# Three tiles of features loaded ahead and the fourth in mid-run, with store slots of 87 instead of 65 pairs

## The chip, the core and the metric

The kernel runs on one core of a Trainium2 chip. The time is that of one execution on the device, in microseconds. The core has TensorE (PE, matrix products), ScalarE (ACT), VectorE (DVE), GpSimd (POOL), SyncE (SP, which here only issues transfers) and 16 DMA engines that move data between the main memory and the on-chip memory of 128 partitions.

## The reference

`r_x` has shape (512, 40, 128) and `W` (128, 128), both float32. Each of the 40 feature rows is projected, and then all 780 pairs (i, j) with i < j are multiplied element by element:

```python
proj = jnp.einsum('bnd,ed->bne', x, W)
out = proj[:, PAIR_I, :] * proj[:, PAIR_J, :]      # (512, 780, 128)
```

The input is 10.5 MB and the output 204.5 MB.

## The kernel before

The 512 rows are four tiles of 128, one row per partition. For each tile, `feats` holds 40 features of 128 numbers per partition. PE turns two features at a time (`turn`, L125) into PSUM, ACT copies them to `x_turned` (L174), PE multiplies them with the turned weights (`project`, L134), and ACT writes the result over the raw features in `feats` (L180). Such a pair of features is a group; there are 20 per tile, from the last features to the first.

DVE multiplies. The 780 pairs are ordered by i and then by j, so all pairs with one i and neighbouring j are one instruction (L197): feature i broadcast, times the features j to j + count - 1. The pairs are cut into chunks of 65, worked from the end of the list to its beginning, because the last features are projected first. A chunk fills one of three slots, `products0` to `products2`; where a chunk's edge lies within one i, that i's instruction is split in two. After a chunk DVE raises `chunk_ready`, SP issues one store of the slot (L107), and the store's landing raises `stored` of the slot, for which DVE waits before it fills that slot again (L196, L212). The first tile's chunks are written out instruction by instruction; the other three tiles are one loop body on DVE, `Fori(1, tiles)`, with the tile's number in a register.

SP issues everything in this order: the first tile in three loads, of features 36 to 39, 28 to 35 and 0 to 27 (L99), the other three tiles in one load each (L101), and then the 48 stores in the order of the chunks, each behind its wait (L106). PE waits for the parts of the first tile one by one, and then once for all three other tiles (L157), before it works on the second. All loads and stores are in one queue, q1. In what follows, tile 0 is the first and tile 3 the fourth.

Of the kernel before, what the change touches and what calls it, by code (L numbers as in the profile page):

```python
# [5 lines left out]
P = 128  # L6
FEATURES = 40
DIM = 128
PAIRS = FEATURES * (FEATURES - 1) // 2
FIRST_PAIR = [i * (FEATURES - 1) - i * (i - 1) // 2 for i in range(FEATURES)]  # L10

GROUP = 2
# [4 lines left out]
FIRST_LOADS = [(36, 40), (28, 36), (0, 28)]  # L17


SLOTS = 3  # L20
CHUNK = 65
CHUNKS = PAIRS // CHUNK
ROUNDS = CHUNKS // SLOTS

assert CHUNKS * CHUNK == PAIRS and ROUNDS * SLOTS == CHUNKS
assert GROUPS * GROUP == FEATURES and GROUPS % 2 == 0 and GROUP <= BANK_FEATURES


def group_range(group):
    return FEATURES - (group + 1) * GROUP, FEATURES - group * GROUP  # L30


def group_of(i):
    return (FEATURES - 1 - i) // GROUP


def chunk_range(k):
    return PAIRS - (k + 1) * CHUNK, PAIRS - k * CHUNK


def chunk_rows(low, high):

    rows = []
    for i in reversed(range(FEATURES - 1)):
        a, b = max(low, FIRST_PAIR[i]), min(high, FIRST_PAIR[i + 1])
        if a < b:
            rows.append((i, i + 1 + a - FIRST_PAIR[i], b - a, a - low))
    return rows


def pairwise_products(nc, x, w, out):
    fp32 = mybir.dt.float32
    ALU = mybir.AluOpType
    tiles = x.shape[0] // P
    assert x.shape[0] == tiles * P and 2 <= tiles <= 4

    with ExitStack() as ctx:  # L57
        def sbuf(name, shape):
            return ctx.enter_context(nc.sbuf_tensor(name, shape, fp32))

        def psum(name, shape):
            return ctx.enter_context(nc.psum_tensor(name, shape, fp32))

        def sem(name):
            return ctx.enter_context(nc.semaphore(name))


        feats = sbuf("feats", [P, tiles, FEATURES, DIM])
        products = [sbuf(f"products{s}", [P, CHUNK, DIM]) for s in range(SLOTS)]
        x_turned = [sbuf(f"x_turned{k}", [DIM, GROUP, P]) for k in range(2)]  # L70
        w_in = sbuf("w_in", [DIM, DIM])
        w_turned = sbuf("w_turned", [DIM, DIM])
        identity = sbuf("identity", [P, P])

        turned_ps = [psum(f"turned_ps{k}", [DIM, BANK_FEATURES, P]) for k in range(2)]
        proj_ps = [psum(f"proj_ps{k}", [P, BANK_FEATURES, DIM]) for k in range(2)]
# [3 lines left out]
        first_loaded = [sem(f"first_loaded{k}") for k in range(len(FIRST_LOADS))]  # L80

        tiles_loaded = sem("tiles_loaded")
        identity_zeroed = sem("identity_zeroed")
        identity_made = sem("identity_made")
        w_in_ps = sem("w_in_ps")
# [4 lines left out]
        proj_ready = sem("proj_ready")  # L90
        chunk_ready = sem("chunk_ready")
        stored = [sem(f"stored{s}") for s in range(SLOTS)]

        block = ctx.enter_context(nc.Block())

        @block.sync
        def _(sp):
            for k, (a, b) in enumerate(FIRST_LOADS):
                sp.dma_start(feats[:, 0, a:b, :], x[0:P, a:b, :]).then_inc(first_loaded[k], 16)  # L99
            for tile in range(1, tiles):  # L100
                sp.dma_start(feats[:, tile, :, :], x[tile * P:(tile + 1) * P, :, :]).then_inc(tiles_loaded, 16)  # L101

            for tile in range(tiles):
                for k in range(CHUNKS):
                    low, high = chunk_range(k)
                    sp.wait_ge(chunk_ready, tile * CHUNKS + k + 1)  # L106
                    sp.dma_start(out[tile * P:(tile + 1) * P, low:high, :],  # L107
                                 products[k % SLOTS][:, :, :]).then_inc(stored[k % SLOTS], 16)

            for slot in range(SLOTS):  # L110
                sp.wait_ge(stored[slot], 16 * tiles * ROUNDS)
# [8 lines left out]
        @block.tensor  # L120
        def _(pe):
            def turn(tile, group):
                a, b = group_range(group)
                for n in range(a, b):
                    last = pe.transpose(turned_ps[group % 2][:, n - a, :], feats[:, tile, n, :], identity[:, :])  # L125
                last.then_inc(group_turned, 1)

            def project(before, group):
                pe.wait_ge(x_turned_ready, before + (group + 1))
                if group >= 2:  # L130

                    pe.wait_ge(proj_ready, before + (group - 1))
                for k in range(GROUP):
                    last = pe.matmul(proj_ps[group % 2][:, k, :], x_turned[group % 2][:, k, :], w_turned[:, :],  # L134
                                     start=True, stop=True)
                last.then_inc(group_projected, 1)

            def last_banks_left(before):
                pe.wait_ge(proj_ready, before + GROUPS)

            pe.wait_ge(identity_made, 1)
            pe.wait_ge(w_loaded, 16)
            pe.transpose(w_ps[:, :], w_in[:, :], identity[:, :]).then_inc(w_in_ps, 1)  # L143

            starts = {group_of(b - 1): k for k, (a, b) in enumerate(FIRST_LOADS)}
            pe.wait_ge(first_loaded[0], 16)
            turn(0, 0)
            pe.wait_ge(w_ready, 1)
            for group in range(1, GROUPS):
                if group in starts:  # L150
                    pe.wait_ge(first_loaded[starts[group]], 16)
                turn(0, group)
                project(0, group - 1)
            project(0, GROUPS - 1)
            last_banks_left(0)

            pe.wait_ge(tiles_loaded, 16 * (tiles - 1))  # L157
            for tile in range(1, tiles):
                turn(tile, 0)
                for group in range(1, GROUPS):  # L160
                    turn(tile, group)
                    project(tile * GROUPS, group - 1)
                project(tile * GROUPS, GROUPS - 1)
                last_banks_left(tile * GROUPS)

        @block.scalar
        def _(act):
            act.dma_start(w_in[:, :], w).then_inc(w_loaded, 16)
            act.wait_ge(w_in_ps, 1)
            act.copy(w_turned[:, :], w_ps[:, :]).then_inc(w_ready, 1)  # L170

            def carry_turned(tile, group):
                act.wait_ge(group_turned, tile * GROUPS + group + 1)
                act.copy(x_turned[group % 2][:, :, :], turned_ps[group % 2][:, 0:GROUP, :]).then_inc(x_turned_ready, 1)  # L174

            def carry_projected(tile, group):

                a, b = group_range(group)
                act.wait_ge(group_projected, tile * GROUPS + group + 1)
                act.copy(feats[:, tile, a:b, :], proj_ps[group % 2][:, 0:GROUP, :]).then_inc(proj_ready, 1)  # L180

            for tile in range(tiles):
                carry_turned(tile, 0)
                for group in range(1, GROUPS):
                    carry_turned(tile, group)
                    carry_projected(tile, group - 1)
                carry_projected(tile, GROUPS - 1)

        @block.vector
        def _(dve):  # L190
            def multiply_chunk(tile, k, seen):

                for i, j, count, place in chunk_rows(*chunk_range(k)):
                    if group_of(i) >= seen:
                        seen = group_of(i) + 1
                        dve.wait_ge(proj_ready, tile * GROUPS + seen)  # L196
                    last = dve.tensor_tensor(  # L197
                        products[k % SLOTS][:, place:place + count, :],
                        feats[:, tile, i:i + 1, :].broadcast_to([P, count, DIM]),
                        feats[:, tile, j:j + count, :], ALU.mult)  # L200
                last.then_inc(chunk_ready, 1)
                return seen

            seen = 0
            for k in range(CHUNKS):
                if k >= SLOTS:
                    dve.wait_ge(stored[k % SLOTS], 16 * (k // SLOTS))
                seen = multiply_chunk(0, k, seen)
            with dve.Fori(1, tiles) as tile:  # L209
                seen = 0  # L210
                for k in range(CHUNKS):
                    dve.wait_ge(stored[k % SLOTS], 16 * ROUNDS * tile + 16 * (k // SLOTS))  # L212
                    seen = multiply_chunk(tile, k, seen)


# [19 lines left out]
```

## Time and profile before

| | |
|---|---|
| median of 3 runs | 505.68 us (505.66 to 505.83) |
| the profiled execution | 505.62 us |
| its span | 503.8 us |
| DVE busy | 433.6 us (86%) |
| PE, ACT busy | 63.4 us (13%), 54.2 us (11%) |
| queue q1, share of 16 DMA engines | 99.3% |
| bytes moved | 215.11 MB, 427 GB/s over the span |

The span is the stretch from the first to the last instruction of one profiled execution; what lies around it is 1.8 us. Busy shares say how full an engine is, not whether anyone waits for it. "Landing" is the moment at which a transfer's last completion count arrives. In the slices each digit is the busy share of a fortieth of the span (12.6 us), in tenths. A window's DMA share and rate are coarse where the window is short, since a packet is counted as a whole; that is why a share can stand above 1.

### The profile page before, as it was taken

How to read it: one execution, taken by the hardware profiler on the slowest of the kernel's cores; microseconds unless marked ns; L12 is line 12 of the kernel's file. 1: busy time of each engine (PE TensorE's matmuls, PEld its weight loads, DVE VectorE, ACT ScalarE, POOL GpSimd, SP SyncE). 2: the span in 40 equal slices, each digit the busy share in tenths (PEclk: the TensorE clock that was granted, in tenths of full speed). 3: DMA queues.
4: the chain of work that ended last, by engine and by line, in shares of the span. 5: the costliest groups of instructions: out<-in, count | busy, mean ns of one | idle time of the engine just before them, and what ended most of it. 6: DMA issues, size and time to landing. Idle time of an engine off the chain costs nothing.

```text
span 503.8 us, 1684 instructions
## 1 busy us (share of the span) xinstructions
PE 63.4 (13%) x481; PEld 57.6 (11%) x481; DVE 433.6 (86%) x196; ACT 54.2 (11%) x162; POOL 0.7 (0%) x6
## 2 busy tenths in 40 slices
PE   6659993000000000000000000000000000000000
PEld 5648982000000000000000000000000000000000
DVE  3987899899899989998898999899899989998930
ACT  5638982000000000000000000000000000000000
POOL 0000000000000000000000000000000000000000
PEclk9969997555555555555555555555555555555555
DMA  8999999999999999999999999999999999999997
GB/s 356 424 403 441 427 424 429 447 428 425 434 444 428 428 433 444 428 428 431 447 428 428 431 447 428 428 431 441 433 428 428 436 439 431 428 428 439 433 433 312
DMA packets 7926, 215.11 MB, mean 427 GB/s; under 512 B 880, under 2 KB 1008, under 8 KB 1264
## 3 DMA queue, kind: packets, MB, share of 16 engines
q1 hardware_dynamic: 7776, 214.96, 99.3%
q8 instruction: 4, 0.07, 0.0%
q10 hardware_dynamic: 144, 0.07, 0.0%
q14 instruction: 2, 0.02, 0.0%
HBM read 10.55 MB, written 204.47 MB: 427 GB/s over the span
## 4 chain that ended last, share of the span: by engine, by line
DMA 62%; DVE 25%; issue 5%; DVEq 2%; PE 1%; ACT 0%
DMA out_dram<-products 62%; DVE products L197 25%; DVEq L57 2%; DMA w_in<-in_L_rec_W_dram 1%; PE proj_ps L134 0%; PE turned_ps L125 0%; DVEq L197 0%; DVEq L196 0%; DVEq L209 0%; PE w_ps L143 0%; ACT feats L180 0%; DVEq L212 0%
## 5 line engine op out<-in xcount | busy, mean ns | idle before, releaser
L197 DVE TENSOR_TENSOR products<-feats 128x1280 f32 (+36 forms) x196 | 433.6, 2275 | 49.2 <-DMA out_dram<-products 41.1
L134 PE MATMUL proj_ps<-w_turned,x_turned 128*128 128x128 f32 x320 | 54.7, 295 | 0.6 <-ACT x_turned L174 0.5
L134 PEld LDWEIGHTS proj_ps<-w_turned,x_turned 128*128 128x128 f32 x320 | 43.3, 197 | 5.3 <-ACT x_turned L174 2.1
L125 PE MATMUL turned_ps<-identity,feats 128*128 128x128 f32 x160 | 31.7, 285 | 11.3 <-DMA feats<-in_r_x_dram 10.3
L174 ACT COPY x_turned<-turned_ps 128x256 f32<-128x256 f32 x80 | 30.0, 377 | 12.3 <-PE turned_ps L125 12.1
L180 ACT COPY feats<-proj_ps 128x256 f32<-128x256 f32 x80 | 29.8, 373 | 10.0 <-PE proj_ps L134 4.7
L125 PEld LDWEIGHTS turned_ps<-identity,feats 128*128 128x128 f32 x160 | 20.9, 148 | 12.3 <-issue 10.5
L170 ACT ACT_TABLE_LOAD x1 | 1.3, 1283 | 1.2 <-PEq L224 1.2
L143 PE MATMUL w_ps<-identity,w_in 128*128 128x128 f32 x1 | 0.4, 447 | 4.2 <-DMA w_in<-in_L_rec_W_dram 4.2
L143 PEld LDWEIGHTS w_ps<-identity,w_in 128*128 128x128 f32 x1 | 0.2, 182 | 4.2 <-issue 4.2
L170 ACT COPY w_turned<-w_ps 128x128 f32<-128x128 f32 x1 | 0.3, 266 | 2.3 <-PE w_ps L143 2.3
L117 POOL TENSOR_SCALAR_AFFINE_SELECT identity<-identity 128x128 f32<-128x128 f32 x1 | 0.3, 294 | 0.2 <-POOL identity L115 0.2
L115 POOL MEMSET identity<- 128x128 f32 x1 | 0.2, 204 | 0.3 <-POOLq L224 0.3
L224 POOL MEMSET const-bfloat16-1.0<- 128x1 bf16 x1 | 0.1, 102 | 0.0
L224 POOL MEMSET const-uint8-127<- 128x1 uint8 x1 | 0.1, 102 | 0.0
L224 POOL MEMSET const-float32-1.0<- 128x1 f32 x1 | 0.1, 99 | 0.0
L224 POOL MEMSET const-float32-0.0<- 128x1 f32 x1 | 0.1, 98 | 0.2 <-issue 0.2
## 6 DMA issues: line engine op xcount, KB each, us to landing
out_dram<-products SPq DMA_DIRECT2D x48, 4160.0 KB, 20.5
feats<-in_r_x_dram SPq DMA_DIRECT2D x3, 2560.0 KB, 19.5
feats<-in_r_x_dram SPq DMA_DIRECT2D x1, 1792.0 KB, 8.3
feats<-in_r_x_dram SPq DMA_DIRECT2D x1, 512.0 KB, 4.3
feats<-in_r_x_dram SPq DMA_DIRECT2D x1, 256.0 KB, 3.2
w_in<-in_L_rec_W_dram ACTq DMA_DIRECT2D x1, 64.0 KB, 3.3
```

The source lines that it names most:

```text
L57: with ExitStack() as ctx:
L115: pool.memset(identity[:, :], 0.0).then_inc(identity_zeroed, 1)
L117: pool.affine_select(out=identity[:, :], in_=identity[:, :], compare_op=ALU.not_equal, fill=1.0, base=0, pattern=[[-1, P]], channel_multip ...
L125: last = pe.transpose(turned_ps[group % 2][:, n - a, :], feats[:, tile, n, :], identity[:, :])
L134: last = pe.matmul(proj_ps[group % 2][:, k, :], x_turned[group % 2][:, k, :], w_turned[:, :], start=True, stop=True)
L143: pe.transpose(w_ps[:, :], w_in[:, :], identity[:, :]).then_inc(w_in_ps, 1)
L170: act.copy(w_turned[:, :], w_ps[:, :]).then_inc(w_ready, 1)
L174: act.copy(x_turned[group % 2][:, :, :], turned_ps[group % 2][:, 0:GROUP, :]).then_inc(x_turned_ready, 1)
L180: act.copy(feats[:, tile, a:b, :], proj_ps[group % 2][:, 0:GROUP, :]).then_inc(proj_ready, 1)
L197: last = dve.tensor_tensor(products[k % SLOTS][:, place:place + count, :], feats[:, tile, i:i + 1, :].broadcast_to([P, count, DIM]), feats ...
L224: nc = _bacc.Bacc("TRN2", target_bir_lowering=False, num_devices=1)
```

## The change

`feats` now has three buffers instead of four. Tile 0 is in buffer 0, tile 1 in buffer 2, tile 2 in buffer 1, and tile 3 in buffer 0 again, once tile 0's features are no longer read. SP loads tiles 0 to 2 ahead of the stores, and tile 3 behind the last store of tile 1; that store's wait says that DVE is done with tile 1, so also with tile 0. PE waits for the two tile loads together, and has a wait of its own for tile 3. The buffers of the slots grow to 87 pairs, a tile has nine chunks, the first of which has 84 pairs (780 = 84 + 8 x 87), and all together there are 36 stores instead of 48. The bytes are the same. In DVE's loop the buffer is `tile * -1 + BUFFERS`, worked out in registers.

```diff
+BUFFERS = 3
 SLOTS = 3
-CHUNK = 65
-CHUNKS = PAIRS // CHUNK
+CHUNK = 87
+CHUNKS = -(-PAIRS // CHUNK)
...
 def chunk_range(k):
-    return PAIRS - (k + 1) * CHUNK, PAIRS - k * CHUNK
+    low = (CHUNKS - 1 - k) * CHUNK
+    return low, min(PAIRS, low + CHUNK)
...
-        feats = sbuf("feats", [P, tiles, FEATURES, DIM])
+        feats = sbuf("feats", [P, BUFFERS, FEATURES, DIM])
+        buffer_of = [0] + [BUFFERS - tile for tile in range(1, tiles)]
...
-            for tile in range(1, tiles):
-                sp.dma_start(feats[:, tile, :, :], x[tile * P:(tile + 1) * P, :, :]).then_inc(tiles_loaded, 16)
+            for tile in range(1, BUFFERS):
+                sp.dma_start(feats[:, buffer_of[tile], :, :],
+                             x[tile * P:(tile + 1) * P, :, :]).then_inc(tiles_loaded, 16)
             for tile in range(tiles):
                 for k in range(CHUNKS):
                     low, high = chunk_range(k)
                     sp.wait_ge(chunk_ready, tile * CHUNKS + k + 1)
                     sp.dma_start(out[tile * P:(tile + 1) * P, low:high, :],
-                                 products[k % SLOTS][:, :, :]).then_inc(stored[k % SLOTS], 16)
+                                 products[k % SLOTS][:, 0:high - low, :]).then_inc(stored[k % SLOTS], 16)
+                if tile == 1:
+                    sp.dma_start(feats[:, 0, :, :],
+                                 x[BUFFERS * P:tiles * P, :, :]).then_inc(last_tile_loaded, 16)
...
-            pe.wait_ge(tiles_loaded, 16 * (tiles - 1))
+            pe.wait_ge(tiles_loaded, 16 * (BUFFERS - 1))
             for tile in range(1, tiles):
+                if tile == BUFFERS:
+                    pe.wait_ge(last_tile_loaded, 16)
                 turn(tile, 0)
...
                     last = dve.tensor_tensor(
                         products[k % SLOTS][:, place:place + count, :],
-                        feats[:, tile, i:i + 1, :].broadcast_to([P, count, DIM]),
-                        feats[:, tile, j:j + count, :], ALU.mult)
+                        feats[:, buffer, i:i + 1, :].broadcast_to([P, count, DIM]),
+                        feats[:, buffer, j:j + count, :], ALU.mult)
...
-                    seen = multiply_chunk(tile, k, seen)
+                    seen = multiply_chunk(tile, tile * -1 + BUFFERS, k, seen)
```

On DVE, in tile 0, the first chunk ends and the second begins here in the kernel before (128 elements are one pair; `products0` is the first slot):

```order
L197 TENSOR_TENSOR products0<-feats 128x1024
L197 TENSOR_TENSOR products0<-feats 128x1152
L197 TENSOR_TENSOR products0<-feats 128x1280 x2
L197 TENSOR_TENSOR products1<-feats 128x128
L197 TENSOR_TENSOR products1<-feats 128x1536
L197 TENSOR_TENSOR products1<-feats 128x1664
```

And here in the changed one:

```order
L213 TENSOR_TENSOR products0<-feats 128x1152
L213 TENSOR_TENSOR products0<-feats 128x1280
L213 TENSOR_TENSOR products0<-feats 128x1408
L213 TENSOR_TENSOR products0<-feats 128x1536
L213 TENSOR_TENSOR products0<-feats 128x768
L213 TENSOR_TENSOR products1<-feats 128x896
L213 TENSOR_TENSOR products1<-feats 128x1792
```

The edge moves from inside i = 28 to inside i = 26, so 13 instructions stand ahead of the first store instead of 11.

On SP, the transfers ahead of the first stores in the kernel before (128x5120 is one tile's features, 128x8320 a slot of 65 pairs):

```order
L99 DMA feats<-in_r_x_dram 128x3584
L101 DMA feats<-in_r_x_dram 128x5120 x3
L107 DMA out_dram<-products0 128x8320 [waits chunk_ready]
L107 DMA out_dram<-products1 128x8320 [waits chunk_ready]
L107 DMA out_dram<-products2 128x8320 [waits chunk_ready]
```

In the changed kernel, the same place, and the place behind the last store of tile 1:

```order
L107 DMA feats<-in_r_x_dram 128x3584
L109 DMA feats<-in_r_x_dram 128x5120 x2
L116 DMA out_dram<-products0 128x10752 [waits chunk_ready]
L116 DMA out_dram<-products1 128x11136 [waits chunk_ready]
...
L116 DMA out_dram<-products1 128x11136 [waits chunk_ready]
L116 DMA out_dram<-products2 128x11136 [waits chunk_ready]
L120 DMA feats<-in_r_x_dram 128x5120
L116 DMA out_dram<-products0 128x10752 [waits chunk_ready]
```

One tile load has moved from ahead of all stores to behind the eighteenth of 36, and it stands there without a wait of its own.

## Rows read from the trace of the kernel before

**Rows 1.** The page: span, DMA slices, queue q1 (packets, MB, share), main memory.
```profile
span 503.8 us, 1684 instructions
...
DMA  8999999999999999999999999999999999999997
...
q1 hardware_dynamic: 7776, 214.96, 99.3%
...
HBM read 10.55 MB, written 204.47 MB: 427 GB/s over the span
```

**Rows 2.** The page: the chain that ended last, by engine.
```profile
DMA 62%; DVE 25%; issue 5%; DVEq 2%; PE 1%; ACT 0%
```

**Rows 3.** The waits: total us, times, longest us.
```profile
DVE products L197 <- DMA out_dram<-products: 41.1, 42, 5.4
SPq L111 <- DMA out_dram<-products: 20.2, 1, 20.2
```

**Rows 4.** The timeline to 75 us (start, duration): DVE, SP's stores, PE's tile 1.
```profile
8.28 27.40 DVE L197 TENSOR_TENSOR products<-feats 128x256 f32<-128x256 f32 x21 [0.77 <-ACT feats L180]
41.04 9.03 DVE L197 TENSOR_TENSOR products<-feats 128x1920 f32<-128x1920 f32 x4 [5.36 <-DMA out_dram<-products]
...
17.61 52.40 SPq L107 DMA_DIRECT2D out_dram<-products  x6
...
31.31 1.09 PE L125 MATMUL turned_ps<-identity,feats 128*128 128x128 f32 x4 [10.34 <-DMA feats<-in_r_x_dram]
```

**Rows 5.** The timeline's end on DVE: chunk 47.
```profile
473.89 8.89 DVE L197 TENSOR_TENSOR products<-feats 128x3328 f32 x2 [0.88 <-DMA out_dram<-products]
```

**Rows 6.** Windows: us, length, busy of PE, PEld, DVE, ACT, POOL, clock, DMA share, GB/s.
```profile
84.00:500.00 416.00, 0.00 (x0) 0.00 (x0) 366.37 (x160) 0.00 (x0) 0.00 (x0) 0.50 1.00 433
```

**Rows 7.** The transfers of 10 to 20 us, then of 140 to 440 us.
```profile
DMA packets 226, 4.30 MB, mean 430 GB/s; under 512 B 16, under 2 KB 16, under 8 KB 16
...
q1 hardware_dynamic: 226, 4.30, 100.0%
...
DMA packets 4381, 129.83 MB, mean 433 GB/s; under 512 B 480, under 2 KB 480, under 8 KB 480
...
q1 hardware_dynamic: 4381, 129.83, 100.3%
```

**Rows 8.** DVE's multiplies by shape: busy us, mean ns of one.
```profile
L197 DVE TENSOR_TENSOR products<-feats 128x4992 f32<-128x4992 f32 x1 | 5.4, 5353 | 0.0
L197 DVE TENSOR_TENSOR products<-feats 128x1280 f32<-128x1280 f32 x5 | 7.4, 1486 | 1.7 <-DMA out_dram<-products 1.7
```

**Rows 9.** Line L101, the three tile loads.
```profile
L101 SPq DMA_DIRECT2D feats<-in_r_x_dram x3: 432/445/652, 2.1 to 3.1; - x3
...
DMA to landing us min/median/max: 13.9/19.5/28.1
```

**Rows 10.** The timeline's first load, and windows around its first bytes.
```profile
0.74 1.33 SPq L99 DMA_DIRECT2D feats<-in_r_x_dram  x3
...
1.60:1.80 0.20, 0.00 (x0) 0.00 (x0) 0.00 (x0) 0.20 (x1) 0.00 (x0) 1.00 0.48 61
```

**Rows 11.** The timeline of PE: its last matmuls of tile 3.
```profile
78.13 1.38 PE L134 MATMUL proj_ps<-w_turned,x_turned 128*128 128x128 f32 x8
```

**Rows 12.** Windows around the third tile load's end.
```profile
20.00:24.00 4.00, 0.96 (x7) 0.58 (x5) 4.00 (x3) 0.95 (x3) 0.00 (x0) 1.00 1.06 450
24.00:28.00 4.00, 0.00 (x0) 0.00 (x0) 4.00 (x4) 0.00 (x0) 0.00 (x0) 0.57 1.04 340
28.00:32.00 4.00, 0.69 (x4) 0.72 (x4) 4.00 (x2) 0.00 (x0) 0.00 (x0) 0.50 1.04 448
...
22.00:32.00 10.00, 0.69 (x4) 0.72 (x4) 10.00 (x6) 0.00 (x0) 0.00 (x0) 0.63 1.04 403
```

**Rows 13.** Windows at the end.
```profile
500.00:501.00 1.00, 0.00 (x0) 0.00 (x0) 0.00 (x0) 0.00 (x0) 0.00 (x0) 0.50 0.24 100
501.00:502.00 1.00, 0.00 (x0) 0.00 (x0) 0.00 (x0) 0.00 (x0) 0.00 (x0) 0.50 0.16 67
```

More of the change, by code:

```diff
@@ L17 @@
 FIRST_LOADS = [(36, 40), (28, 36), (0, 28)]
+BUFFERS = 3
 SLOTS = 3
-CHUNK = 65
-CHUNKS = PAIRS // CHUNK
+CHUNK = 87
+CHUNKS = -(-PAIRS // CHUNK)
 ROUNDS = CHUNKS // SLOTS
-assert CHUNKS * CHUNK == PAIRS and ROUNDS * SLOTS == CHUNKS
+assert ROUNDS * SLOTS == CHUNKS
 assert GROUPS * GROUP == FEATURES and GROUPS % 2 == 0 and GROUP <= BANK_FEATURES
@@ L54, in pairwise_products @@
     tiles = x.shape[0] // P
-    assert x.shape[0] == tiles * P and 2 <= tiles <= 4
+    assert x.shape[0] == tiles * P and tiles == BUFFERS + 1
     with ExitStack() as ctx:
@@ L190, in _, with multiply_chunk @@
         def _(dve):
-            def multiply_chunk(tile, k, seen):
+            def multiply_chunk(tile, buffer, k, seen):
                 for i, j, count, place in chunk_rows(*chunk_range(k)):
```

8 lines of the change are left out of this document (5 added, 3 removed).

## The prediction

> **What bounds the kernel now.** I read the page first, then the chain of waits, the waits by themselves, the timelines, and last the transfers in stretches. The slices of the DMA line stand at 9 from the second to the last but one, and the queue q1 holds 16 DMA engines for 99.3% of the span at 427 GB/s [rows 1]. 10.55 MB are read and 204.47 MB written, and neither kernel can do with less. The chain that ended last names the stores with 62% and DVE with 25%, but that split says only that DVE stands between two landings [rows 2]: DVE waits 42 times for a store to land, together 41.1 us, and SP waits at the end for the last store, 20.2 us after it was issued [rows 3]. So DVE always has a free slot late and a full slot early. In the steady part it starts a chunk when a slot lands, needs 9.03 us [rows 4], and the two stores still queued last twice as long. From the start on chunk 3 at 41.04 [rows 4] to the start on chunk 47 at 473.89 [rows 5] there are 44 landings: 432.85 / 44 = 9.84 us per store of 4.26 MB, that is 433 GB/s, the same as the windows give for 84 to 500 us [rows 6]. The time is thus bytes over the rate of the DMA engines, plus the start before the first byte, plus any moment in which the queue is empty or slow. The change is worth what it does to these, and nothing on DVE, PE or ACT counts unless it empties the queue.
>
> **Cost per packet.** Each of the 128 partitions gives one packet per transfer, so each of the 16 engines has 8 per store. From 10 to 20 us only tile loads run: 4.30 MB are 210 packets of 20,480 B, and 10 x 16 x 1.000 = 160 us of engine time make 762 ns each. From 140 to 440 us only stores: 129.83 MB are 3,901 packets of 33,280 B, 300 x 16 x 1.003 = 4,814 us, 1,234 ns each [rows 7]. The difference is 472 ns for 12,800 B, or 36.9 ns per 1,000 B, and 762 - 20.48 x 36.9 leaves 7 ns that don't depend on the size (the completion counts are in it). Before, an engine handles 48 x 8 = 384 store packets, after 36 x 8 = 288, with the same bytes in them. 96 x 7 ns = 0.7 us less. The shares are rounded to 0.1% and the megabytes to 0.01, which moves the 7 ns by some 4 either way, so the term lies between 0.3 and 1.1 us. I take -0.7. The Trainium skill (DMA: Bandwidth & Descriptors, Why small descriptors are slow) states a fixed overhead of about 3 cycles per packet between the read and the write side, and the same page puts the fabric at 850 MHz; by that the 96 packets would be worth an estimated 0.3 us. The trace's 7 ns are about twice that, and the forecast goes by the trace; neither can be told from no change by itself.
>
> **The start.** The first store now has 84 pairs and so comes later, while one tile load fewer lies ahead of it. DVE: 4,992 elements (39 pairs) take 5,353 ns and 1,280 (10 pairs) 1,486 [rows 8], so 133.3 ns per pair. The 21 instructions from 8.28 on cover chunks 0 to 2 but for the first pair, 194 pairs, in 27.40 us [rows 4]: (27.40 - 25.87) / 21 = 0.073 us per instruction on top. Chunk 0 of 84 pairs ends at 8.28 + 83 x 0.1333 + 12 x 0.073 = 20.2 us (by the same sum 65 pairs end at 17.5; SP issued at 17.61, [rows 4]). The queue ahead of it runs out when the second tile load is done: the three were issued at 2.11 to 3.1 us and landed after 13.9, 19.5 and 28.1 us [rows 9], so the second near 2.6 + 19.5 = 22.1. A transfer issued at 0.74 moves its first bytes between 1.60 and 1.80 [rows 10], 1.0 us later. The store's first bytes could thus go at 21.2 to 21.4, while the last load packets are still under way. The fastest engines may stand for some tenths: +0.2, between 0 and +1. Chunk 1 (87 pairs, 6 instructions) ends at 20.2 + 11.6 + 0.4 = 32.3 and its bytes can go at 33.3; the 84-pair store needs 8 x (1,234 + 9.73 x 36.9) ns = 12.7 us and ends at about 34.1. Chunk 2 ends at 44.3, its queue at 47.3. From there DVE gains about 1.1 us per chunk (12.05 against 8 x 1.65 = 13.2 us), until the slots hold it back as before. The cover is thinnest at chunk 1, 0.8 us.
>
> **The steady part.** Longer chunks keep the balance: a slot lands, DVE needs 0.9 + 12.05 us, the two queued stores last 26.4. The loop body has other register operations ahead of its multiplies (the buffer index counts down); even one microsecond per chunk for them would be hidden by the 12 us left. The multiplies of a tile fall from 49 to 46: 3 x 0.073 us less, hidden too. Cost 0, and 0 from both sides as long as this cover stands.
>
> **The moved load.** It holds the same 2.62 MB and 6.1 us wherever it runs, so moving it costs nothing by itself. SP issues it behind chunk 8 of the second tile, without a new wait; a tile load holds SP for 0.45 us [rows 9], while two full stores are queued, and the next store is ready 12 us later. By the sums above it is issued near 232, its bytes go at about 257 to 263 us (21.4 + 2 x 117.8), and it lands near 264. PE and ACT need it for tile 3 only; they took 31.3 to 79.5 us for three tiles [rows 4, 11], 16 us each, so tile 3 is ready near 281, and DVE starts on it near 355. PE's new wait has nothing behind it but tile 3, and no one asks for that for 70 us. DVE's slot lands 6.1 us later behind the load, but then the load is queued with the stores, so nothing runs dry.
>
> **The slow end of the loads.** This is the term that I can't fix. The third tile load landed near 3.1 + 28.1 = 31.2, 9.1 us after the second, where the second came 6.1 after the first [rows 9]. From 24 to 28 us only 340 GB/s were moved with the engines full, where the windows beside show 450 and 448 [rows 12]. Over 22 to 32 us it is 403 against 430 for the loads before, 10 x 27 / 430 = 0.63 us; over the four microseconds alone 4 x 90 / 430 = 0.84. I take 0.8 us as the price of one such end. What causes it the rows don't say: the store waiting in the queue behind, the position or the moment. Afterwards there are two ends of loads before stores, at 21 us with the store barely queued, and at 263 with stores ahead and behind. So the term lies between -0.8 (gone) and +1.6 (paid three times, with the entry into the load). I take 0: paid once, at the moved load, which looks like the old end.
>
> **The tail.** The engines are full to 500 us [rows 6] and then drop to 0.24 and 0.16 in the next two microseconds, with the end of the span at 503.8 [rows 1, 13]: they finish unevenly, and a last store of 87 pairs is no different, since the queue is fed until its last packet. 0, at most 0.4 (one packet of 1.65 instead of 1.23 us).
>
> **Sum.** The profiled execution took 505.62 us, of which 503.8 are span; the median is 505.68. 505.62 - 0.7 + 0.2 + 0 = 505.1 us, 0.1% less than before. About 0.2%, 1.0 us, is what a measurement of this kernel can tell from no change.
>
> **Rivals.**
> - *The slow end vanishes.* For it: stores moved at full rate throughout [rows 6, 7], the slowness struck only the third tile load, between 24 and 31 us, and in that stretch now only stores run. Against: the moved load has a full queue behind it as the old one had. 505.1 - 0.8 = 504.3 us; on the slowest engine the old end cost up to 9.1 - 6.1 = 3.0 us, so this side may reach 503.5. Chance 0.28.
> - *The moved load is paid at both sides (slower).* Place: the engines change from stores to loads at 257 us and back at 263. Price: each change like the old one, 0.8 us, and the end at 21 us still paid: 505.1 + 1.6 = 506.7. It decides from the point where the stretch around the load lasts over 1.5 us longer than 6.1. For it: reads next to stores are the only slow stretch of the trace. Against: one change at the start was all there was, and nothing shows that entering a load costs. Chance 0.14.
> - *The queue runs dry at the start.* The first bytes of the 84-pair store would have to come after 23.2 us, 2.9 after its issue, to cost 1.7 us and show as slower: 506.6. The 1.0 us of the first transfer speaks against it. Chance 0.04. The Trainium skill (Perfetto Trace Analysis, DMA Optimizations) says that smaller transfers may let some start sooner, which here would speak for slots of 65; the landing of the second load near 22.1 says that nothing could start sooner.
> - *Stores have a price of their own.* If each of the 12 stores fewer saved a fixed cost, the time would fall by 12 times that. The landings lie 9.84 us apart at 433 GB/s, so no more than hundredths are left between them. At 0.1 us each: 503.9. Chance 0.02. [...]
>
> **How the numbers follow.** The forecast has 0.52: its terms add up to between -0.9 and +0.9 us around the old time, nearly all within 0.2%. The first and the last rival fall below 504.67 and make faster 0.30; the two slow ones with a little of the forecast's upper end make slower 0.16; 0.54 is left for the same. The range from 503.8 to 506.7 takes in the vanished end and the load paid twice, and leaves out the rarer sides of each.
>
> **What would show it.** In the profile after: the stores at about 13.15 us from landing to landing and 433 GB/s; DMA slices at 9 without a dip near 21 and 34 us; first store issued at 20.2 to 20.4; PE's long wait for the last tile, off the chain; DVE's waits for landings fewer and longer. A rate of 340 GB/s near 260 us would confirm the forecast's slow end, full rate at 21 and at 260 the first rival. A DMA slice below 9 in the middle, or a DVE waiting for PE or ACT in tile 3, would make the prediction wrong.

## The result, and the profile after

The changed kernel takes 506.78 us (median of 16 runs, 506.31 to 507.31), the kernel before 505.69 us on the same chip (505.55 to 505.90). The ratio is 1.0021, 95% interval 1.0014 to 1.0027: slower by 0.2%, 1.09 us, where 505.1 us and a small gain were forecast. The runs also spread over 1.0 us instead of 0.35.

The profiled execution took 507.06 us. The page after, as in [rows 1, 3]:

```profile
span 505.3 us, 1657 instructions
...
DMA  8999999999999999999999999999999999999997
...
q1 hardware_dynamic: 6048, 214.96, 99.1%
```

The queue is still full nearly everywhere, with the same bytes. The slices hide where 1.5 us of span went. The two places show in short windows (columns as in [rows 6]). First the start:

```profile
20.00:21.00 1.00, 1.00 (x10) 0.85 (x8) 1.00 (x3) 0.92 (x4) 0.00 (x0) 1.00 0.86 369
21.00:22.00 1.00, 0.78 (x5) 0.52 (x4) 1.00 (x2) 0.57 (x3) 0.00 (x0) 1.00 1.53 639
22.00:23.00 1.00, 0.01 (x1) 0.04 (x1) 1.00 (x1) 0.20 (x1) 0.00 (x0) 1.00 0.26 86
23.00:24.00 1.00, 0.76 (x5) 0.52 (x6) 1.00 (x2) 0.56 (x2) 0.00 (x0) 1.00 1.41 602
```

A packet counts in the window in which it starts, so such rows only tell that all engines start together: at 21.8 us, and again 1.6 us later. The trace also has the start, the length and the size of every packet; joining each packet's end to the next start gives the work of the 16 engines one by one. By these packet records most engines were through with the loads at 20.8 to 21.3 us and 14 of them began the first store at 21.82 to 21.96. The mean engine stood for 0.7 us. The timeline of SP and DVE has the reason:

```profile
20.98 48.04 SPq L116 DMA_DIRECT2D out_dram<-products  x5
...
8.49 0.89 DVE L213 TENSOR_TENSOR products<-feats 128x256 f32<-128x256 f32 x2 [0.99 <-ACT feats L196]
9.77 1.43 DVE L213 TENSOR_TENSOR products<-feats 128x512 f32<-128x512 f32 x2 [0.39 <-ACT feats L196]
```

The store goes out at 20.98 instead of 20.2 us, since DVE waits for ACT at its second and fourth instruction. The second place is the moved load (its line, then windows around it):

```profile
L120 SPq DMA_DIRECT2D feats<-in_r_x_dram x1: 1258/1258/1258, 233.0 to 233.0; - x1
...
DMA to landing us min/median/max: 36.0/36.0/36.0
```

```profile
250.00:256.00 6.00, 0.00 (x0) 0.00 (x0) 6.00 (x4) 0.00 (x0) 0.00 (x0) 0.50 1.05 453
256.00:262.00 6.00, 0.00 (x0) 0.00 (x0) 4.61 (x3) 0.00 (x0) 0.00 (x0) 0.50 0.93 346
262.00:268.00 6.00, 0.00 (x0) 0.00 (x0) 6.00 (x3) 0.00 (x0) 0.00 (x0) 0.50 1.04 372
268.00:274.00 6.00, 4.77 (x27) 4.31 (x27) 4.56 (x3) 2.72 (x8) 0.00 (x0) 0.63 0.97 419
```

It was issued at 233.0 (forecast 232) and landed at 269.0 (forecast 264). The four windows have a mean of 398 GB/s where the stores have 433: 24 x 35 / 433 = 1.9 us, with the engines full. In the packet records both sides are slow: the last store packet ahead of the load takes about 2.4 us on 14 engines instead of 1.646 (together 0.7 us per engine, below called the entry), and the last three of eight load packets take up to 2.25 us instead of 0.76 (1.1 us per engine, the exit). At the old place, the third load's end [rows 12], the same records give 1.0 us, and no slow store packets. The load's late landing costs nothing further: DVE waits for neither PE nor ACT in tile 3.

```profile
DVE products L213 <- DMA out_dram<-products: 37.3, 27, 9.3
DVE products L213 <- ACT feats L196: 8.6, 3, 7.2
```

Against [rows 3], DVE's waits for landings are fewer and one is long (9.3 us, behind the load); DVE's waits for ACT all lie in tile 0.

### The profile page after: what moved, and what is told of

It is laid out like the page before. It is cut to its first block, busy times and chain, and to the rows that moved or that the text cites. A ratio compares the mean times of both kernels' runs of the same rounds, so it can differ in the third digit from the quotient of the medians.

```text
span 505.3 us, 1657 instructions
## 1 busy us (share of the span) xinstructions
PE 64.1 (13%) x481; PEld 58.5 (12%) x481; DVE 431.4 (85%) x184; ACT 54.3 (11%) x162; POOL 0.7 (0%) x6
## 4 chain that ended last, share of the span: by engine, by line
DMA 51%; DVE 36%; issue 5%; DVEq 2%; PE 1%; ACT 0%
DMA out_dram<-products 50%; DVE products L213 36%; DVEq L62 1%; DMA w_in<-in_L_rec_W_dram 1%; PE proj_ps L148 1%; PE turned_ps L138 0%; DVEq L213 0%; DVEq L225 0%; PE w_ps L157 0%; ACT feats L196 0%; DVEq L212 0%; DVEq L228 0%
## 5 line engine op out<-in xcount | busy, mean ns | idle before, releaser
L213 DVE TENSOR_TENSOR products<-feats 128x768 f32 (+48 forms) x184 | 431.4, 2417 | 45.9 <-DMA out_dram<-products 37.3
```

Of the source, the lines that this page charges most:

```text
L213: last = dve.tensor_tensor(products[k % SLOTS][:, place:place + count, :], feats[:, buffer, i:i + 1, :].broadcast_to([P, count, DIM]), fea ...
```

## The experiments

Theory T: load and stores changing places in the queue cost engine time beyond the bytes. Rival S: the load is free of that, and the loss comes from the larger slots. P, C, F and L, further down, are explained where they are first tested. All times are medians, beside runs of the kernel before on the same chip (505.76 to 505.78 us).

**1. The load taken away, slots of 87 and of 65; the load with slots of 65.**

```diff
-                if tile == 1:
-                    sp.dma_start(feats[:, 0, :, :], x[BUFFERS * P:tiles * P, :, :]).then_inc(last_tile_loaded, 16)
...
-                    pe.wait_ge(last_tile_loaded, 16)
+                    pe.wait_ge(chunk_ready, 2 * CHUNKS)
```

The second has `CHUNK = 65` as well; the third is the changed kernel with `CHUNK = 65` alone.

> The changed kernel without the load of tile 3 (PE starts on tile 3 when the last chunk of tile 1 is done and works on what the buffer holds, so the fourth quarter of the output is of other data). Theory T: each turn of the queue costs engine time of its own, about 0.7 us where a load follows stores and 1.0 us where stores follow a load with a store already queued behind it. Then the load takes its bytes' 6.1 us and 1.7 us of turns with it: 506.8 - 7.8 = 499.0 us. Rival S: the load in mid-run costs its bytes alone, and the changed kernel loses by its slots of 87 (late first store, coarser pieces): 506.8 - 6.1 = 500.7 us.

> The same without the load of tile 3, with slots of 65 pairs. T: like the kernel before less 6.1 us, the slow end of the early loads kept, 499.6 us, so 0.6 us more than with slots of 87 (0.5 us of packets and the 1.0 us slow end against the 0.7 us in which the queue stood empty at the start). S: slots of 65 are better by at least 1.1 us, so less than the run with 87 by that much.

> The changed order of loads with the slots of the kernel before (65 pairs). T: the early slow end is paid as before, and both turns of the moved load come on top: 505.7 + 1.7 = 507.4 us; in the profile the last store packets ahead of the load and the last load packets are slow. S: 505.7 us, as the kernel before.

Measured 498.96 (ratio 0.9867, 0.9851 to 0.9882), 499.47 (0.9878, 0.9863 to 0.9893) and 506.37 us (1.0015, 1.0006 to 1.0024). The load's bytes are 2.62 MB, 6.02 us at the 435 GB/s of the window from 274 to 300 us in the changed kernel's trace. With slots of 87 it costs 506.78 - 498.96 = 7.8 us, 1.8 beyond its bytes. With 65 it costs 6.9, 0.9 beyond. Without it the larger slots are better, by 0.5 us. S falls: slots and start together are worth 498.96 - (505.76 - 6.02) = -0.8 us, and the load's +1.8 turns that into the loss. T's 507.4 for the third was 1.0 too much, so the price isn't a constant. The 1.8 us is a net price: without the load the store packets also stay longer to the end (0.7 us per engine after 257 us, against 0.1 in the changed kernel; experiment 7 comes to this), and the slowest engine ends 1.0 us after the mean one instead of 1.9. That it equals the 0.7 and 1.1 us of the packet records is in part chance.

**2. The load in two parts.** Features 20 to 39 at the old place, 0 to 19 four stores later, PE waiting for both.

> The changed kernel with the load of tile 3 cut in two: features 20 to 39 behind the last store of tile 1, features 0 to 19 four stores later. T: two turns more, 506.8 + 1.7 = 508.5 us, and two slow places in the profile. S: the same bytes, 506.8 us.

507.20 us (1.0024, 1.0013 to 1.0036), not to be told from the changed kernel, and 1.3 less than T had said. The windows around the second part say why:

```profile
308.00:314.00 6.00, 0.00 (x0) 0.00 (x0) 6.00 (x3) 0.00 (x0) 0.00 (x0) 0.50 1.05 453
314.00:320.00 6.00, 0.00 (x0) 0.00 (x0) 4.84 (x3) 0.00 (x0) 0.00 (x0) 0.50 0.91 380
320.00:326.00 6.00, 4.96 (x22) 4.58 (x23) 6.00 (x2) 2.29 (x7) 0.00 (x0) 0.50 1.03 447
```

Their mean is 427 GB/s, 0.3 us short. The first part paid the full price (0.7 and 1.0 us in the packet records), the second no entry and an exit of 0.1.

**3. The start.** The first store in two, 45 pairs and 39, the slot's waits raised by 16:

```diff
+            low, high = chunk_range(0)
+            sp.wait_ge(first_half, 1)
+            sp.dma_start(out[0:P, high - FIRST:high, :], products[0][:, high - low - FIRST:high - low, :]).then_inc(stored[0], 16)
+            sp.wait_ge(chunk_ready, 1)
+            sp.dma_start(out[0:P, low:high - FIRST, :], products[0][:, 0:high - low - FIRST, :]).then_inc(stored[0], 16)
...
```

> The changed kernel with the first store cut in two: the first 45 pairs go as soon as they are ready (about 14.7 us), the other 39 as before. The engines no longer stand between the second tile load and the first store (0.7 us each in the profile of the changed kernel). If a store queued behind a load makes the load's end slow (theory T), part of that comes back there, up to 1.0 us: 506.1 to 507.1 us. If a queued store does nothing to the load: 506.1 us.

And in the kernel before, `sp.wait_ge(tiles_loaded, 48)` ahead of all stores:

> The kernel before, but SP waits until all loads have landed before it issues the first store, so that no store stands in the queue behind a load. T: the third tile load's slow end is gone, it lands near 28.2 instead of 31.2 us; the queue then stands empty for about 1.6 us: 505.7 - 1.0 + 1.6 = 506.3 us. Rival: the slow end belongs to the third load itself (its place or its moment): it still lands near 31.2 us, 507.3 us.

The first took 506.68 us (1.0018, 1.0009 to 1.0027): the gap is gone and a slow end of 0.9 us has come at the second load (16 to 24 us, at 420 and 353 GB/s):

```profile
16.00:20.00 4.00, 4.00 (x35) 3.84 (x35) 4.00 (x4) 3.57 (x12) 0.00 (x0) 1.00 1.07 420
20.00:24.00 4.00, 2.35 (x17) 1.71 (x16) 4.00 (x4) 2.10 (x7) 0.00 (x0) 1.00 0.95 353
```

In the second the three loads land after 14.0, 19.6 and 26.1 us, the last against 28.1 in [rows 9]:

```profile
DMA to landing us min/median/max: 14.0/19.6/26.1
```

Its packet records have no slow end at all. So it is the store behind the load that makes the load's end slow: a store moved ahead brought it, a store held back removed it. The size isn't fixed by that: with slots of 65 and two tile loads ahead (the second kernel of experiment 1) the end cost 0.5 us. The kernel that waits took 507.84 us (1.0046, 1.0032 to 1.0060), 1.5 more than T had said. The empty queue was longer (2.8 us per engine, not 1.6), and its store packets had become longer (experiment 7).

**4. Packets.** `CHUNK = 26` in the kernel before.

> The kernel before with slots of 26 pairs: 120 stores instead of 48, 960 store packets per DMA engine instead of 384, the same bytes. The step between equal stores on the earliest engine (9.83 us at 65 pairs) leaves 5.5 ns per packet above the bytes at 435.2 GB/s, so 576 x 5.5 ns = 3.2 us more, 508.9 us. By the 7 ns of the prediction: 509.7. By the 3 cycles of the Trainium skill, an estimated 3.5 ns: 507.7.

511.96 us (1.0121, 1.0105 to 1.0136), 6.2 us more, or 10.8 ns for each of the 576 packets more per engine. From 140 to 440 us:

```profile
DMA packets 10780, 127.63 MB, mean 425 GB/s; under 512 B 1192, under 2 KB 1192, under 8 KB 1192
```

That is 425 GB/s against 433 in [rows 7]. All three forecasts were low. But the 10.8 ns is no price for the change's 96 packets. In the packet records an engine most often starts a packet of 20,480 B 758 ns after the last (before, 10 to 20 us) and one of 33,280 B 1,228 ns after (140 to 440 us), which leaves about 6 ns beside the bytes, and by the same line 13,312 B need 495 ns. Here 494 ns is the most frequent step, but the mean is 501, so about half of what a packet costs here beside its bytes is a slowness of this kernel's own, whose cause no run shows. Nor does the run part a price per packet from one per store, since each store has eight packets per engine. For the change's 96 packets some 0.5 to 0.6 us are left.

**5. Six loads more in the kernel before**, of tile 0 again, behind the stores of chunks 2 and 7 in tiles 1 to 3 (`if tile >= 1 and k in (2, 7,): sp.dma_start(feats[:, 0, 0:40, :], x[0:P, 0:40, :])`, with a count of its own).

> The kernel before with six further loads of a whole tile (tile 0 again, into its buffer that nobody reads any more), two in each of the tiles 1 to 3, in the midst of the stores. The bytes of one are 6.02 us. If a load between stores costs its bytes alone: 505.7 + 36.1 = 541.8 us. T: each costs 0.9 (as with slots of 65) to 1.8 us (as with 87) of turns besides: 547.2 to 552.6 us.

546.81 us (1.0811, 1.0797 to 1.0826), so 6.84 us each, 0.8 beyond the bytes. T's 0.9 to 1.8 us was close only at its lower end. None of the six had an entry (at most 0.03 us per engine), and their exits cost 0.1 to 0.7.

**6. Place and source.** P says that the price hangs on the place between two tiles, C that it comes from rows read for the first time; F is a fixed price. The load behind the sixth store of tile 2; behind the last store of tile 0; at the old place, but of tile 0's rows; and with one small load of tile 3's rows at the start.

> The changed kernel with the load of tile 3 behind the sixth store of tile 2 instead of behind the last of tile 1. In the profiles so far the entry into the load was slow (0.4 to 0.7 us per engine) only where it stood between two tiles, and the slow exit was smaller in the last third of a tile (0.15 to 0.3 us) than elsewhere (0.6 to 1.1). Theory P (the price hangs on the place): 506.8 - 0.7 - 0.8 = 505.3 us. Rival F (a fixed price of some 1.7 us for load and stores changing places): 506.8 us.

> The same load behind the last store of tile 0, the other place between two tiles. P: the slow entry (0.7 us) and the slow exit (1.0 us) are there as in the changed kernel, 506.8 us. If the slow entry belonged to the moment near 257 us or to what lies around it, not to the place between tiles: 506.1 us or less.

> The changed kernel, but the load in mid-run reads the input rows of tile 0 again instead of those of tile 3 (the fourth quarter of the output repeats the first). Theory C (first read): the slow turns come from reading a part of the input that was not read before; six reloads of tile 0 had no slow entry and small exits. Then 506.8 - 1.3 = 505.5 us. Theory T without C: which rows are read doesn't matter, 506.8 us.

> The changed kernel with one small load more at the start that reads 512 B of each row of tile 3 (feature 0) into the unused third slot. C: the mid-run load then finds its rows read before, the slow entry is gone: 505.5 to 506.1 us with 0.2 us for the small load. T without C: 506.9 us.

506.80 (1.0022, 1.0013 to 1.0032), 506.09 (1.0007, 0.9998 to 1.0016), 506.83 (1.0021, 1.0012 to 1.0030) and 506.85 us (1.0020, 1.0011 to 1.0029). Both P and C fall. Slow entry and exit are there at every place and with every source; here with the load behind the sixth store of tile 2:

```profile
328.00:334.00 6.00, 0.00 (x0) 0.00 (x0) 6.00 (x3) 0.00 (x0) 0.00 (x0) 0.50 1.05 453
334.00:340.00 6.00, 0.00 (x0) 0.00 (x0) 4.05 (x2) 0.00 (x0) 0.00 (x0) 0.50 0.84 291
340.00:346.00 6.00, 0.00 (x0) 0.00 (x0) 6.00 (x3) 0.00 (x0) 0.00 (x0) 0.50 1.04 380
```

The load behind tile 0, at 138 us instead of 257, is 0.7 us better than the changed kernel, which P had excluded. That is a hint at what follows.

**7. The store in time, and longer packets.** In the kernel before, tile 3's load in two parts, and SP waits for the first part only:

```diff
-            for tile in range(1, tiles):
+            for tile in range(1, tiles - 1):
...
+            sp.dma_start(feats[:, tiles - 1, 16:40, :], x[(tiles - 1) * P:, 16:40, :]).then_inc(most_loaded, 16)
+            sp.dma_start(feats[:, tiles - 1, 0:16, :], x[(tiles - 1) * P:, 0:16, :]).then_inc(tiles_loaded, 16)
+            sp.wait_ge(most_loaded, 16)
...
```

> The kernel before, with tile 3's load cut in two (features 16 to 39, then 0 to 15), and SP waits for the first part's landing (near 26 us) before it issues the first store, so that the store enters the queue about 1 us before the loads end. T: a store that has stood in the queue only briefly makes nearly no slow end (none in the changed kernel, 1.0 us where it stood there for 9 us), and the queue hardly runs empty: 505.7 - 0.9 + 0.1 (8 packets more per engine) = 504.9 us. Rival: any queued store costs the full slow end: 505.8 us.

505.54 us (0.9996, 0.9987 to 1.0005): the slow end is gone, the queue stands for 0.5 us, and still next to nothing is won (T had said 504.9). The stores themselves had become slower. The transfers of 200 to 480 us, where all of these kernels only store, first of the kernel before, then of this one:

```profile
DMA packets 4090, 121.21 MB, mean 433 GB/s; under 512 B 448, under 2 KB 448, under 8 KB 448
```

```profile
DMA packets 4078, 120.81 MB, mean 431 GB/s; under 512 B 448, under 2 KB 448, under 8 KB 448
```

0.3% fewer bytes in 280 us are 0.9 us. In the packet records the kernel before has 1,232 ns for 5,125 of its 6,144 store packets, this one for 1,838; most of the others take 1,233 to 1,241 ns. By all its packets the mean engine ends 1.2 us later than in the kernel before, but the slowest ends at the same time, 502.9 us: it is 0.5 us behind the mean instead of 1.8. With the slow end gone, 12 of the 16 engines start a packet within 0.2 us (200.68 to 200.88 us); in the kernel before the closest 12 take 0.4 us (201.13 to 201.52). Theory L, lockstep: engines in step hinder each other, engines somewhat out of step don't. The tests: 15 tiny loads over 1 to 15 rows ahead of the first store, meant to give the 16 engines from 15 packets down to none (1 KB rows, in this kernel and in the changed one; 1.5 KB rows), and one reload of tile 0 behind the third store of tile 1 in this kernel.

```diff
+            for n in range(1, 16):
+                sp.dma_start(scratch[0:n, n - 1, :, :], x[0:n, 0:2, :]).then_inc(staggered, 16)
...
```

> The kernel before with the store in time (as in e13), plus 15 tiny loads over 1, 2, ... 15 rows of 1 KB into a scratch tile, queued behind the tile loads: DMA engine 0 gets 15 packets, engine 14 one, engine 15 none, so the 16 engines start their stores some 45 ns apart. Theory L (lockstep): where all engines start their store packets at the same moments, a packet takes 1,236 to 1,239 ns instead of 1,232, about 0.4 us per 100 us, and the slow end of a load used to scatter them. Then 505.5 - 1.8 + 0.4 = 504.1 us. Rival: the longer packets have another cause (traffic, the store's late start): 505.9 us.

> The changed kernel with the same 15 tiny loads ahead of the first store (into the third slot, which is still unused). They fill part of the 0.7 us in which the engines stood, and scatter them from 22 us on instead of from 257 us. L: 506.8 - 0.5 (lockstep up to 257 us) - 0.3 = 506.0 us; the turns of the moved load (1.7 us) stay. Rival: 506.8 us or more.

> As e15, with rows of 1.5 KB instead of 1 KB in the 15 tiny loads, so that the engines start their stores some 65 ns apart instead of 45. L (lockstep makes store packets longer): the packets' excess over 1,232 ns falls further below that of e15, which had about half of e13's; the time stays bound by the one engine that came 1.7 us behind the others in e15, 507 us or a little more. Rival: the excess stays as in e15.

> The kernel before with the store in time (e13, whose engines run in lockstep) and one reload of tile 0 behind the third store of tile 1. Theory L2: the slow entry (0.4 to 0.7 us) strikes engines in lockstep, and after the turn they are scattered, so the store packets behind it fall to 1,232 ns. Then the entry is in the profile near 180 us, and the time is 505.5 + 6.0 + 1.6 - 1.3 = 511.8 us. Rival: with slots of 65 and rows read before, there is no slow entry, as in e9: exit 0.6 us only, 512.2 us if the packets stay long, and 510.9 if they fall.

They took 507.00 (1.0025, 1.0014 to 1.0035), 507.81 (1.0045, 1.0032 to 1.0059) and 507.35 us (1.0032, 1.0020 to 1.0043); the first is slower than either forecast and the second 1.8 us slower than L's 506.0. In the kernel with the store in time, the excess over 1,232 ns between 200 and 480 us fell from 1.1 us per engine to 0.75 with rows of 1 KB and 0.6 with 1.5 KB (121.04 MB in both, against 120.81). But the tiny loads had a price of their own: the first store packets behind them were 0.7 to 0.8 us longer per engine, and the last engine came 2.0 to 2.3 us behind the mean. As a remedy this failed; as a test of L it points the right way, no more.

The reload is the clear one: 513.49 us (1.0154, 1.0140 to 1.0168). It had the slow entry (0.6 us) and exit (1.1 us), with slots of 65, in mid-tile, on rows read before:

```profile
172.00:178.00 6.00, 0.00 (x0) 0.00 (x0) 5.25 (x2) 0.00 (x0) 0.00 (x0) 0.50 0.99 384
178.00:184.00 6.00, 0.00 (x0) 0.00 (x0) 5.65 (x2) 0.00 (x0) 0.00 (x0) 0.50 1.08 389
```

Experiment 5 had the same load at the same place without an entry; its store packets ahead of the load were not longer. And behind the reload, the rate of the kernel before is back:

```profile
DMA packets 4104, 121.24 MB, mean 433 GB/s; under 512 B 461, under 2 KB 461, under 8 KB 461
```

The excess of the store packets is 0.5 us per engine from 40 to 90 us, 0.3 from 90 to 165, and 0.01 per 100 us behind the reload. The price beyond the bytes was 513.49 - 505.54 - 6.02 = 1.9 us, much as in the changed kernel; my 511.8 had counted a gain behind it that did not reach the slowest engine (1.7 us behind the mean again, instead of 0.5).

Over all the runs with a load between stores, the entry goes with the packets ahead of it. In eleven loads the store packets of the 28 us before were longer by 2.8 to 7.1 ns on average, and the entry was 0.4 to 0.8 us. In seven (the six of experiment 5 and the second part of experiment 2) they were longer by at most 0.2 ns, and it was at most 0.03 us. L itself fares worse. With the load at 138 us, 12 engines start within 0.23 us at 201 us, as close as in the kernel with the store in time, and the packets are longer by only 0.15 ns; in the changed kernel the closest 12 take 0.5 us at 200 us and 0.4 us at 280, and the packets are longer by 4.5 ns at the first place and by 0.1 to 0.4 from 350 us on. So that packets run long or short for hundreds of us, and that a whole-tile load between stores makes them short, is shown; that being in step is the cause is not.

**8. The best of both**: the changed kernel with the load behind the sixth store of tile 2 and the first store in 78 and 6 pairs.

> The changed kernel with the load of tile 3 behind the sixth store of tile 2, and the first store cut in 78 and 6 pairs, so that its first bytes are due near 20.5 us, just ahead of the loads' end. P and T: 505.3 - 0.5 (of the 0.7 us of an empty queue) = 504.8 us, below both kernels. F and a full slow end for any queued store: 506.9 us.

506.38 us (1.0012, 1.0003 to 1.0021), where P with T had 504.8 and F 506.9. The start was mended (no gap, no slow end), and the load kept its full price. No version here is clearly faster than the kernel before.

## Why the prediction was wrong

**What bounds the kernel** was right: the time is bytes over the rate of the engines plus empty and slow moments. DVE, PE, ACT and the loop's registers cost nothing, and the cover in the steady part held.

**Cost per packet** had the right sign. -0.7 us was forecast. The steps between undisturbed packets give about 6 ns each (experiment 4), so -0.5 to -0.6 us; no run isolates the term. The slots' side as a whole (packets, start, the old slow end gone, longer packets) measured -0.8 us in experiment 1.

**The start** was mis-sized. The term was +0.2 us and the profile has 0.7. The sum for chunk 0 took DVE's first instructions as unhindered because they were nearly so in [rows 4]; the waits for ACT, 0.99 and 0.39 us, vary with how fast the first loads land. In the six kernels here with a whole first store of 84 pairs directly behind the second tile load it was issued between 20.38 and 21.07 us, and the engines stood for 0.2 us in the first case and 0.9 in the last. The kernel before issues at 17.61 with the queue full until 28 us, so it swallows that. The wider spread of the changed kernel doesn't come from this alone: the third kernel of experiment 1, whose queue never stood empty, spread over 1.2 us (506.10 to 507.26).

**The slow end of the loads** is the step that failed. "I take 0: paid once, at the moved load, which looks like the old end." It is paid at both sides: entry 0.7 and exit 1.1 us instead of 1.0 at the old place, and by the runs the moved load took 1.8 us beyond its bytes. The rival with this mechanism had its place and its entry right and 14%; its third payment, at 21 us, did not come, since the first store entered the queue too late to slow the load; an empty queue of nearly the same size stood in its place. So it was by luck that its 506.7 us lay next to the measured time.

**The steady part** had a cost that nobody had named. From 40 us to the moved load, the changed kernel's store packets are longer by 0.7 us per engine in all, those of the kernel before by 0.3; behind the load it is 0.1, and the kernel before gathers 0.4 us late, from 300 us on. Up to 257 us the difference is +0.5 us, over the whole run from 40 us on +0.2, and from 22 to 40 us it is another +0.2. It explains, in part, why the same load at 138 us is 0.7 us cheaper.

**The tail** was right for these two: the slowest engine ends 1.9 us after the mean one in the changed kernel and 1.8 in the kernel before. It isn't a constant, though (0.5 us with the store in time), so a gain or a loss of the mean engine need not reach the time.

The 505.7 - 0.8 (slots, start, old slow end) + 1.8 (moved load) = 506.7 us of experiment 1 is no test of this account, since both terms are taken from the same run and must add up. The packet records are one: by them the mean engine ends 1.5 us later: packets -0.6, empty queue +0.7, entry and exit 1.8 - 1.0 = +0.8, longer store packets +0.4, slower first loads +0.2, together +1.5 (this execution, 507.06 us, was itself 0.3 above the median).

What stays open is why a store behind a load slows the load's end, what makes store packets long or short, and why only long ones are followed by an entry. That a slow end alone sets them right isn't so: the kernel with the first store in two had one at 20 us, its packets were longer by 4.5 ns ahead of the moved load, and the entry was 0.55 us all the same.

## What to carry to other kernels

Where the DMA queue is the bound, moving a load costs more than its bytes: count a price for each side on which it touches stores, here 0.8 to 1.9 us in all for 2.6 MB. Loads that stand ahead of all stores touch them once. A first store that is only just in time is a risk, since an early wait of any engine then empties the queue; work out its time with the early waits that can grow, not only with those of one trace. When a slow place is removed and the time stays, look at the rate of the undisturbed stretch in both traces, and at how far the last engine is behind the mean, before doubting the removal.

## What was not expected of the hardware

- A load with a store queued behind it had a slow end of 1.0 us per engine (28.1 us to landing); with no store queued it had none (26.1 us). The same load between stores had an entry only where the store packets ahead of it ran long.
- The same stores moved 120.81 MB in 280 us in one kernel and 121.21 MB in another, with packets of 1,234 to 1,241 ns instead of 1,232; a single whole-tile load between stores switched from one to the other (121.24 MB behind it). The cause is not known.
- Cutting the same bytes into packets of 13 KB instead of 33 KB, 576 more per engine, took 6.2 us more, 10.8 ns for each; the steps between undisturbed packets leave about 6 ns beside the bytes.
- The end is set by the last of 16 engines, 1.8 us behind the mean in the kernel before and 0.5 us in the one with the store in time: the mean engine ended 1.2 us later in the second, the last at 502.9 us in both.
